# Front with parameters loaded first, one product per bias row, and sorts, tables and result biases moved

## What is computed

```
x    = patches @ W_patch + b_patch + pos_embed          # 16x16 patches, 768 numbers each
K0   = sum((x @ W_spinor + b_spinor)**2)
xe   = ((x @ W_coord + b_coord) @ W_embed + b_embed) * K0 + x
h    = layernorm(xe) * gamma + beta;  h = h @ W_out + b_out
K    = ifft(at_roots(Lambda, P, B, C, log_step))        # Cauchy sums over 64 states, 49 roots
h    = h + causal_conv(layernorm(h), K) + D * layernorm(h)
t    = layernorm(h)
h    = h + 2 shared experts(t) + top-2 of 8 routed experts(t)   # 128 -> 512 -> 128, gelu
```

## Time and profile before

| | us |
|---|---|
| three runs: lowest, median, highest | 439.99, 440.13, 445.27 |
| profiled execution, its own time | 444.05 |
| its span (first to last instruction) | 442.1 |
| mean granted TensorE clock in it | 0.883 |

### The profile page before, as it was taken

The page is one execution under the profiler, slowest core; times in us unless marked ns, Lnnn a source line. Parts: engine busy times, 40 slices in busy tenths (PEclk is TensorE's granted clock), DMA queues, the critical chain, the costliest instruction groups (busy, mean ns, idle before and its releaser), DMA issues.

```text
span 442.1 us, 7120 instructions
## 1 busy us (share of the span) xinstructions
PE 364.2 (82%) x2490; PEld 299.8 (68%) x2490; DVE 183.0 (41%) x579; ACT 205.5 (46%) x424; POOL 174.1 (39%) x226
## 2 busy tenths in 40 slices
PE   0596998998967895839899999999999999989400
PEld 0465856666655784739777878988988988988300
DVE  0473485737769202392787221121121121121166
ACT  2660647837351631445563244554454445455153
POOL 7015134255221230062000357767767767654100
PEclk9995799998995697955798899999999999999855
DMA  8962046930010341022003015425435444455185
GB/s 209 265 191 74 16 131 165 312 128 0 1 71 40 122 150 60 1 74 73 0 33 130 19 42 210 159 101 212 156 128 183 161 146 166 172 173 187 29 278 149
DMA packets 22168, 54.38 MB, mean 123 GB/s; under 512 B 4551, under 2 KB 10109, under 8 KB 22137
## 3 DMA queue, kind: packets, MB, share of 16 engines
q1 hardware_dynamic: 17625, 46.25, 31.8%
q0 software_dynamic: 3968, 7.41, 6.0%
q10 hardware_dynamic: 544, 0.33, 0.4%
HBM read 28.10 MB, written 6.93 MB: 79 GB/s over the span
## 4 chain that ended last, share of the span: by engine, by line
PE 52%; issue 15%; DVE 12%; DMA 8%; POOL 4%; POOLq 3%; DVEq 3%; ACT 3%; SPq 1%; ACTq 0%
PE bank L1528 11%; PE bank L1505 11%; PE bank L1515 8%; DMA Xc<-in_x 3%; PE bank L1267 3%; PE bank L1300 3%; DVE dT L848 2%; PE bank L1480 2%; PE bank L1485 2%; PE bank L1486 2%; PE bank L1487 2%; DMA out<-osb 2%; DMA Tt<-kpad 1%; PE bank L1355 1%; PE bank L1563 1%
## 5 line engine op out<-in xcount | busy, mean ns | idle before, releaser
L633 POOL DMA_INDIRECT xg<-yd,take x56 | 54.5, 974 | 64.1 <-DVE give L1186 47.3
L784 ACT ACTIVATE gf<-bank,wb 128x256 f32<-128x256 f32 (+1 forms) x128 | 51.3, 447 | 52.6 <-PE bank L1505 52.6
L640 POOL DMA_INDIRECT rd<-og,give x56 | 55.2, 986 | 41.4 <-DVE og L1200 28.9
L1528 PE MATMUL bank<-wb,gf 128*128 128x128 f32 x448 | 55.4, 275 | 1.0 <-DVE og L1200 1.0
L1505 PE MATMUL bank<-x,wb 128*128 128x256 f32 (+1 forms) x256 | 54.0, 354 | 2.1 <-issue 1.2
L1528 PEld LDWEIGHTS bank<-wb,gf 128*128 128x128 f32 x448 | 53.2, 192 | 1.5 <-DVE og L1200 1.5
L784 ACT ACTIVATE gf<-bank,vcol 128x392 f32<-128x392 f32 x64 | 35.2, 588 | 36.5 <-PE bank L1487 36.5
L1505 PEld LDWEIGHTS bank<-x,wb 128*128 128x128 f32 x256 | 43.3, 191 | 9.3 <-issue 1.4
L1515 PE MATMUL bank<-gf,ws 128*128 128x392 f32 x128 | 44.8, 492 | 0.0
L1193 DVE COPY x<-bank 128x256 f32<-128x256 f32 (+1 forms) x32 | 12.5, 391 | 65.4 <-PE bank L1563 65.3
L1300 PE MATMUL bank<-patchT,Wp 128*128 128x392 f32 x96 | 38.4, 527 | 0.0
(11 more groups left out here) (266 smaller groups left out, 627.7 us busy)
## 6 DMA issues: line engine op xcount, KB each, us to landing
wb<-tab SPq DMA_DIRECT2D x32, 578.0 KB, 3.3
Xc<-in_x SPq DMA_DIRECT2D x12, 784.0 KB, 6.8
rk<-rd SPq DMA_DIRECT2D x8, 392.0 KB
Tt<-kpad SPq DMA_DIRECT2D x8, 300.1 KB
raw<-in_L_ffn_rw SPq DMA_DIRECT2D x1, 2048.0 KB, 10.2
out<-osb SPq DMA_DIRECT2D x8, 196.0 KB
Tt<-kpad SPq DMA_DIRECT2D x2, 600.2 KB
Tt<-kpad SPq DMA_DIRECT2D x1, 1200.5 KB
```

The source lines that it names most:

```text
L633: G.indirect_dma_start(out=xg[i % AHEAD][:, t, :], out_offset=None, in_=yd[:, :], in_offset=bass.IndirectOffsetOnAxis(ap=take[:, at:at + 1 ...
L640: G.indirect_dma_start(out=rd[:, :], out_offset=bass.IndirectOffsetOnAxis(ap=give[:, at:at + 1], axis=0), in_=og[i % 2][:, t, :], in_offse ...
L784: nc.scalar.activation(gf[q % 2][:, o, 0:width(q)], bank[o][:, 0:width(q)], ACT.Gelu, bias=bias1(n, o)).then_inc(act_done, 1)
L1528: last = MM(bank[7][:, D * t:D * (t + 1)], gf[q % 2][:, o, 128 * t:128 * (t + 1)], wb[i % WB][:, FO + F + o * D:FO + F + (o + 1) * D], sta ...
```

## The change

- SP issues `lsraw`, `craw`, `lim` and `tan2` ahead of the first pixels. ACT keeps `ident`, `praw`, `braw` and `lre`. The wait for parameters now counts eight loads, `tan2` among them; VectorE's wait for the ten other loads (`ld_tok`) goes from ahead of `cauchy_b` to the bias rows.
- ACT makes `s2` first, sorts channel 0 of tile 0, squares bT, and begins tile 0; channels 1 and 2 of tile 0 are sorted behind the copies of steps 1 and 3. Channels 0 and 1 of tile 1 are sorted behind the copy of step 5, and channel 2 between the two `xtok` copies.
- TensorE makes the two tables in step 4, behind its projection of step 3, with the bias row a second time at partition 32.
- `bhi` and `blo` become rows 0 and 32 of one operand `bhl` of 33 rows, zero between, and `ones` has 33 rows with ones in rows 0 and 32. `add_bias` is one product. The two b rows are loaded twice for it.
- The copy of `rbb` and its wait (`result_biases`) go behind the eight additions of the convolution.

```
+LOW = 32
...
+            load(lsraw[:, :], log_step.rearrange("(a b) -> a b", b=2), ld_par)
+            load(craw[:, :, :], C_.rearrange("(a b) n t -> a (b n) t", b=2), ld_par)
+            load(lim[:, :], Lambda_im.rearrange("(a b) n -> a (b n)", b=2), ld_par)
+            load(tan2[:, :], c_tan[0:1, :].broadcast_to([128, L]), ld_par)
             for c in range(C):
                 load_x(0, c)
                 if c == 0:
-                    load(lsraw[:, :], log_step.rearrange("(a b) -> a b", b=2), ld_par)
                     load(Wp[:, :, :], W_patch.rearrange("(t p) d -> p t d", p=128), ld_wp)
-            load(tan2[:, :], c_tan[0:1, :].broadcast_to([128, L]), ld_tok)
...
-            load(brow[:, 0, :], rows(b_embed), ld_tok)
-            load(brow[:, 1, :], rows(b_out), ld_tok)
+            for at in (0, LOW):
+                load(brow[at:at + 1, 0, :], rows(b_embed), ld_tok)
+                load(brow[at:at + 1, 1, :], rows(b_out), ld_tok)
...
-            for dst, src in ((praw, P_), (braw, B_), (craw, C_)):
+            for dst, src in ((praw, P_), (braw, B_)):
...
-            for dst, src in ((lre, Lambda_re), (lim, Lambda_im)):
-                act.dma_start(dst[:, :], src.rearrange("(a b) n -> a (b n)", b=2)).then_inc(ld_par, 16)
+            act.dma_start(lre[:, :], Lambda_re.rearrange("(a b) n -> a (b n)", b=2)).then_inc(ld_par, 16)
...
-                    if t == (1 if first else 2):
-                        act.wait_ge(b_ready, k + 1)
-                        nc.scalar.activation(dT[:, :, :], bT[:, :, :], ACT.Square).then_inc(sq_ready, 1)
+                    if t == 2 and not first:
+                        square(k)
...
-                    if t % 2 == 1 and more:
+                    if t in (1, 3) and first:
+                        sort_pixels(0, t // 2 + 1)
+                    if t % 2 == 1 and more and not first:
                         sort_pixels(k + 1, t // 2)
+                    if t == KT - 1 and first:
+                        sort_pixels(1, 0)
+                        sort_pixels(1, 1)
...
+                    if first and half == 0:
+                        sort_pixels(1, C - 1)
...
-            for c in range(C):
-                sort_pixels(0, c)
             act.wait_ge(ls_T, 1)
             nc.scalar.activation(s2[:, :], bank[4][:, 0:HP], ACT.Exp, scale=-1.0).then_inc(s2_ready, 1)
+            sort_pixels(0, 0)
+            square(0)
             tile(0, True, True)
...
+            def result_biases():
                 dve.wait_ge(ld_rbb, 16)
                 V.tensor_copy(tab[:, :, FO + F + FO * D:RW], rbb[:, :, :]).then_inc(biases_in, 1)
...
-            dve.wait_ge(ld_tok, 16 * 9)
...
-            V.memset(ones[:, :].bitcast(F32), 1.0)
-            V.tensor_tensor(brow[:, 0, :], brow[:, 0, :], bank[6][0:1, D:2 * D], ALU.add).then_inc(tok_const, 1)
+            V.memset(ones[:, :].bitcast(F32), 0.0)
+            V.memset(bhl[:, :, :].bitcast(F32), 0.0)
+            dve.wait_ge(ld_tok, 16 * 10)
             dve.drain()
-            V.tensor_copy(bhi[:, :, :], brow[:, :, :])
+            for at in (0, LOW):
+                row = slice(at, at + 1)
+                V.memset(ones[row, :].bitcast(F32), 1.0)
+                V.tensor_tensor(brow[row, 0, :], brow[row, 0, :], bank[6][row, D:2 * D], ALU.add)
             dve.drain()
-            V.tensor_tensor(blo[:, :, :], brow[:, :, :], bhi[:, :, :].bitcast(F32), ALU.subtract).then_inc(bias_ready, 1)
+            for at in (0, LOW):
+                last = V.tensor_copy(bhl[at:at + 1, :, :], brow[at:at + 1, :, :])
+            last.then_inc(tok_const, 1)
+            dve.drain()
+            low_row = slice(LOW, LOW + 1)
+            V.tensor_tensor(bhl[low_row, :, :], brow[low_row, :, :], bhl[low_row, :, :].bitcast(F32), ALU.subtract).then_inc(bias_ready, 1)
...
             dve.drain()
+            result_biases()
...
-                for n, part in enumerate((bhi, blo)):
-                    MM(dst[0:PAIR, :], ones[:, :], part[:, i, :].unsqueeze(1).broadcast_to([1, GP, D]), start=n == 0, stop=False)
+                MM(dst[0:PAIR, :], ones[:, :], bhl[:, i, :].unsqueeze(1).broadcast_to([LOW + 1, GP, D]), start=True, stop=False)
...
+            def embed_tables():
+                pe.wait_ge(wcT_ready, 1)
+                MM(bank[6][:, 0:D], wcT[:, :], we[:, :], start=True, stop=True)
+                MM(bank[6][0:1, D:2 * D], bccol[:, :], we[:, :], start=True, stop=True)
+                MM(bank[6][LOW:LOW + 1, D:2 * D], bccol[:, :], we[:, :], start=True, stop=True, tile_position=(0, LOW)).then_inc(wce_T, 1)
...
+                    if t == KT - 2 and first:
+                        embed_tables()
...
-                    pe.wait_ge(wcT_ready, 1)
-                    MM(bank[6][:, 0:D], wcT[:, :], we[:, :], start=True, stop=True)
-                    MM(bank[6][0:1, D:2 * D], bccol[:, :], we[:, :], start=True, stop=True).then_inc(wce_T, 1)
```

More of the change, by code:

```diff
@@ L284, in tower @@
         wsp = place("wsp", [D, DS], "k")
-        brow = place("brow", [1, 2, D], "su")
+        brow = place("brow", [LOW + 1, 2, D], "su")
         bsp = place("bsp", [PAIR, DS], "k")
@@ L307, in tower @@
         none = place("none", [PAIR, 2 * GP], "k")
-        ones = place("ones", [1, PAIR], "k", F32R)
-        bhi = place("bhi", [1, 2, D], "k", F32R)
-        blo = place("blo", [1, 2, D], "k", F32R)
+        ones = place("ones", [LOW + 1, PAIR], "k", F32R)
+        bhl = place("bhl", [LOW + 1, 2, D], "k", F32R)
         ksb = place("ksb", [L, D], "k")
@@ L677, in sort_pixels, with square @@
                                Xc[c][:, :].rearrange("r (i w j) -> r i w j", i=P, w=NH)).then_inc(x_sorted[c], 1)
+            def square(k):
+                act.wait_ge(b_ready, k + 1)
+                nc.scalar.activation(dT[:, :, :], bT[:, :, :], ACT.Square).then_inc(sq_ready, 1)
             def back(k, half):
@@ L832, in _ @@
             V = nc.vector
-            dve.wait_ge(ld_par, 16 * 7)
+            dve.wait_ge(ld_par, 16 * 8)
             V.tensor_copy(lsrep[:, :, :], lsraw[:, :].unsqueeze(2).broadcast_to([HP, 2, N])).then_inc(lsrep_ready, 1)
@@ L1267, in to_columns @@
                 return TP(dst, src, ident[0:rows_, 0:rows_])
-            pe.wait_ge(ld_par, 16 * 7)
+            pe.wait_ge(ld_par, 16 * 8)
             for i, src in enumerate((praw[:, :, 0], praw[:, :, 1], braw[:, :, 0], braw[:, :, 1], craw[:, :, 0], craw[:, :, 1],
```

## The result

| us | before | changed |
|---|---|---|
| runs | 439.99, 440.13, 441.29, 445.27 | 421.23, 422.45, 427.69, 427.77 |
| median | 440.71 | 425.07 |
| profiled execution, its span | 444.05, 442.1 | 421.23, 419.3 |
| mean granted clock in it | 0.883 | 0.915 |

The ratio is 0.955, with a 95% interval of 0.946 to 0.964: faster by 4.5%. The changed kernel's runs stand in two groups, 421 to 422 and 427.7, and this ratio leaves out the upper one; the two medians by themselves give 0.965. What parts the groups is part of the story.

What follows compares the result with a forecast made beforehand. Bound by TensorE's waits: late parameters and a clock-lowering hole in tile 0, and a convolution hole. Front 11.4, bias products 3.6 and result biases 3.2 sum to 18.2 us off the median 440.13: 422 us, range 415 to 431.

Steps and rivals of the forecast that it cites:

- Loads: Front: four parameter loads ahead of the pixels bring parameters at about 5.5 us, first pixels between 8.5 and 9.4.
- T: When TensorE can start tile 0's patch transposes: 10.2 to 11.1 us, taken 10.6, against 16.06.
- Tile 0: Tile 0's six steps: together about 19 us, TensorE ends at 29.6, embed starts at 30.5 instead of 36.83.
- The bias rows: Ahead of tile 0's embed: VectorE takes 2.8 to 4.5 us, ready at 28.6 to 30.3, just hidden behind projections.
- Clock: Tile 0's embed: without the hole it runs at 2.4 GHz, 4.8 us long, ending at 35.3 against 46.66.
- the first rival: Tile 0's embed: bias rows late, embed still slow, costing 4.5 to 5.3 us, about 427; chance 0.2.
- One product: Bias products: one per bias row instead of a pair saves half a pair each on the path, 3.6 us.
- Result biases: Convolution: rbb's copy behind the additions gains 3.9 us, less 0.7 for the bare copy: 3.2 us.
- A wait in tile 1: Tile 1 waits for a third of its pixels, 3 to 7 us plus a clock drop: 427 to 433; chance 0.1.
- late Toeplitz block: Convolution: a Toeplitz block lands only with rbb, the hole stays, 3 us less gain: 425; chance 0.07.
- Pixels: Tile 0: pixels are the bound, T = 12 and 2 us more; gain 4 to 5 less; chance 0.15.
- The stretch at the lower clock ahead of the experts: Half-clock stretch, 189 to 213 us: its end moves behind the shared experts' first products, slower, 442 to 449; chance 0.03.

## Why the prediction was right, point by point

The forecast was 422 us in 415 to 431; the medians are 425.07 and, once more, 423.62. The mechanisms were those named; the terms have their measured sizes now.

**Loads and T: right.** Parameters at 6.27 (5.5 forecast), first pixels at 9.41 (8.5 to 9.4), T = 11.15 (10.2 to 11.1, taken 10.6). The kernel with parameters behind the pixels lost 9.2 us of this term, and the one with all sorts first shows that the ACT order matters as much: neither half alone moves the embed ahead of before.

**Tile 0: right.** Behind T the embed starts 18.7 us later (19.9 forecast with the copy); the projections end at 28.23 (29.6).

**The bias rows: the forecast's "just hidden" failed, at small cost.** They were ready at 29.07, later than the projections by 0.8, and were what the copy into xT, and with it the embed, waited for. The forecast's own terms did not give "just hidden": 3.0 us for the old steps and five more of 0.15 to 0.4 are 3.75 to 5.0 us, not 2.8 to 4.5; from the end of the tables at 24.76 the rows took 4.3. I had GpSimd's lock hold back the first steps of the chain and not the last, because I had its operations end at 27. They ran from 21.2 to 30.4 and the last but one held the last step, in other executions both casts. The step took 1.57 us beside GpSimd's operation and 0.41 without it. The Trainium skill, "SBUF — State Buffer", section "SBUF: two separate sides", says that a VectorE operation with two inputs in SBUF and a GpSimd operation that reads SBUF contend for one shared port pair, which the first to start holds for its whole instruction; these two durations agree.

**Clock: right in the profiled execution, and the first rival in others.** The embed took 4.88 us at 1.0 there. In two kernels that are the same up to that point, or nearly, it took 9.0 and 9.5, and 7.7 in the one with all sorts first. I gave the slow embed 0.2; it is a matter of the execution. Two of four runs, then two of six, stand at 427. In the four kernels that fill the wait or shorten it no run of 22 is above 423.1, so the long runs depend on TensorE's idle time ahead of the embed; that they are long by the embed's clock fits their steps, but none of them was profiled. The length of the wait does not decide by itself: the clock stayed at 1.00 behind 1.64, 1.61 and 1.33 us of it (the last with the parameters late), and fell behind 2.62, 1.84 and 1.42. This is most likely what puts the medians 1.6 and 3.1 us above 422 while the lower runs are at it.

**One product: the mis-sized term.** 3.6 us forecast by half of a pair; by the rows a product gives 0.23 or 0.43, so the same eight and two products give 8 x 0.23 + 2 x 0.43 = 2.7. The 33 rows cost nothing: 0.40 and 0.23 us for two products, and 0.63 for a pair with one row. The interval from tile 0's statistics to the convolution shrank by 5.2 in the profiles. It has less time at 0.5 (some 3.5 us less in the tiles, 7 less from the last norm on), which I had not counted and which varies with the execution; that the other 2.5 come from there is argued. The run with a second product grew in it by only 1.4, so no run isolates the 2.7.

**Result biases: 3.2 forecast, 2.8 to 4.5 measured** in profiles of the stage (4.5 from before to changed, 4.1 in before alone, 2.8 undone), 1.9 in the median of before alone. The gap came in all three profiles that have the early wait (3.27, 3.00 and 3.50 us); how long the half clock lasts behind it differed (some 7 us, 3 and 3).

**The rivals.** A wait in tile 1 and a late Toeplitz block did not come: in tile 1 TensorE waits for no sort, and Tt costs it 0.6 us at most at once. Pixels do bound the first transposes now, but not at the price of that rival: T is 11.15 and not 12, and ACT never waits for a later third. The stretch at the lower clock ahead of the experts ended where it had, 22 us earlier.

**The sum.** 11.4 + 3.6 + 3.2 = 18.2 was forecast, and 12.3 + 5.2 + 4.5 + 0.8 = 22.8 is between two profiled executions, the first a long one of its kernel and the second a short one. The shortest runs of each give 439.99 to 421.23: 18.8. That the forecast of 422 lies so near is partly luck: the products were put 0.9 too high, while 2.5 us in the tiles and 1.3 in the convolution were not counted, and the long runs moved the median the other way.

## What to carry to other kernels

Look at what TensorE waits for just ahead of a stage, look up the granted clock in the stage, and price the hole with the clock, not with its length: here the embed behind a hole of 3.9 us took 4.5 more, and unused products in the hole ended that embed 3.1 us earlier, though it began 1.4 later. Where a wait stands on one engine ahead of unrelated work (rbb's copy ahead of eight additions), ask who needs what is queued behind it. A time that falls in two groups is worth following: here small operations met GpSimd's long ones or missed them by under a microsecond, and with a wait on the engine that had time to spare, or with the idle time filled, the upper group was not seen again.

## What was not expected of the hardware

- The window rows print a granted 1.00 from 11 to 16 us, in which seven transposes take 1.57 us; from 16.71 they take 0.84. Early in an execution durations tell the level, the printed clock doesn't.
- In the changed kernel the clock stayed at 0.50 from 174.5 to 188.8 us, with TensorE's records back to back. With 6.75 us of wide products ahead of that stage it was 1.00 until about 173.5 and fell behind a wait of 2.10 us.
- An operation on 256 numbers took 0.41 us alone and 1.57 to 1.90 beside one of GpSimd's, two casts 0.58 alone (with the tables late) and 3.10 beside two. Which of them is held changes from execution to execution: where loads, sorts and tables stand as in the changed kernel, the first pixels landed anywhere from 9.41 to 10.21 us and the casts began from 26.36 to 27.38, in the main later with later pixels, while GpSimd's product QT began within 0.05 us of 25.15 each time.
- The same kernel took 440 us on one chip and 475 on another. From tile 0's statistics to the first convolution product the profiles show 96 to 99 us on the second and 95 to 101 elsewhere; behind the shared experts' first product they are some 20 to 37 us longer there.
